# Moving the last value-sum copy ahead of the second layer-norm statistics, regrouping six SBUF tiles, and spreading the top-k over one more cycle

## The reference

```python
xn = _layernorm(x)                                  # first norm
# attention: a second norm with weights, then q, k, v, rotary, softmax, output projection
zn = (xn - mu) * rsqrt(var + LN_EPS) * ln_w + ln_b
q, k, v = rope(proj(zn, Wq, bq)), rope(proj(zn, Wk, bk)), proj(zn, Wv, bv)
attn = softmax(q @ k.T / sqrt(16)); a = xn + (attn @ v) @ Wo.T + bo
# experts: each takes the 256 rows per batch that score highest for it
gating, index = top_k(softmax(xn @ gate_w).T, 256)  # per batch and expert
h = silu(xn[index] @ Wg) * (xn[index] @ Wu)
f = scatter_add((h @ Wd) * gating)
return x + a + f
```

## Time and profile before

| | us |
|---|---|
| median of three runs | 1722.32 |
| lowest, highest | 1722.04, 1726.52 |
| the profiled execution's own time | 1719.68 |
| its span (first to last instruction) | 1717.5 |

### The profile page before, as it was taken

One profiled execution on the slowest core, in us unless ns is written; L12 is line 12 of the kernel. 1 busy time (PEld: TensorE's weight loads), 2 busy tenths in 40 slices (PEclk: granted clock), 3 DMA queues, 4 the chain that ended last, 5 costly groups with the idle time before them and its releaser, 6 DMA issues.

```text
span 1717.5 us, 29029 instructions
## 1 busy us (share of the span) xinstructions
PE 1668.0 (97%) x11128; PEld 946.9 (55%) x11128; DVE 1076.3 (63%) x2351; ACT 1190.9 (69%) x1416; POOL 510.1 (30%) x479
## 2 busy tenths in 40 slices
PE   5799999999999999999999999999999999999997
PEld 4234344334434433433434433368888888888886
DVE  8875486487567467568458658966545555454543
ACT  4698988998898899899898899953333333333322
POOL 3121111101201111112112100046565665656553
PEclk9899999999999999999999999999999999999999
DMA  5635745764674475465465466255353453535332
GB/s 168 175 89 124 140 108 118 173 130 106 156 160 109 120 165 138 108 149 142 118 148 127 113 128 140 46 162 125 68 98 63 93 100 57 99 59 96 65 56 31
DMA packets 113987, 196.08 MB, mean 114 GB/s; under 512 B 20896, under 2 KB 59680, under 8 KB 113696
## 3 DMA queue, kind: packets, MB, share of 16 engines
q1 hardware_dynamic: 83696, 143.01, 36.0%
q0 software_dynamic: 29040, 49.83, 14.9%
q10 hardware_dynamic: 1088, 1.05, 0.2%
HBM read 117.27 MB, written 76.55 MB: 113 GB/s over the span
## 4 chain that ended last, share of the span: by engine, by line
PE 88%; DVE 7%; DMA 2%; issue 1%; POOL 1%; SPq 0%; ACT 0%; DVEq 0%; POOLq 0%; ACTq 0%
PE o_ps L999 26%; PE score L1079 20%; PE score L985 18%; PE side L868 5%; PE score L1091 5%; PE o_ps L1091 3%; PE side L878 3%; PE side L1091 2%; PE side L909 2%; PE score L1066 2%; DVE stats L1128 1%; PE side L852 1%; DMA o_sums<-o_sb 1%; DVE o_sb L1471 1%; DMA probs<-in_wo_t 1%
## 5 line engine op out<-in xcount | busy, mean ns | idle before, releaser
L777 ACT ACTIVATE probs<-score 128x1024 f32<-128x1024 f32 x1024 | 968.6, 1053 | 107.6 <-PE score L985 105.3
L999 PE MATMUL o_ps<-probs,v_ones 128*32 128x512 f32 x4096 | 523.8, 604 | 8.7 <-DVE o_sb L1471 8.6
L985 PE MATMUL score<-q_stack,k_stack 50*128 50x512 f32 x2048 | 391.5, 455 | 4.0 <-issue 3.4
L985 PEld LDWEIGHTS score<-q_stack,k_stack 50*128 50x128 f32 x2048 | 162.8, 185 | 347.9 <-ACT probs L777 305.8
L761 ACT ACTIVATE probs<-score 128x512 f32<-128x512 f32 x128 | 76.5, 598 | 331.1 <-PE score L1079 331.1
L689 POOL DMA_INDIRECT out<-probs,rot x128 | 203.3, 1588 | 211.3 <-DVE probs L1436 182.0
L1421 DVE TENSOR_TENSOR probs<-score,probs 128x512 f32<-128x512 f32 x128 | 88.6, 692 | 209.9 <-PE score L1079 183.1
L999 PEld LDWEIGHTS o_ps<-probs,v_ones 128*32 128x32 f32 x4096 | 92.2, 108 | 209.8 <-issue 139.8
L667 POOL TENSOR_TENSOR square<-qk 128x512 bf16<-128x512 f32 x56 | 77.2, 1407 | 388.1 <-DVE qk L1274 388.1
L1079 PE MATMUL score<-k_stack,q_stack 128*128 128x512 f32 x640 | 158.6, 390 | 0.0
L678 POOL DMA_INDIRECT qk<-xn_rows,rot x128 | 134.0, 1047 | 38.4 <-issue 29.3
(11 more groups left out here) (282 smaller groups left out, 2548.0 us busy)
## 6 DMA issues: line engine op xcount, KB each, us to landing
q_parts<-parts SPq DMA_DIRECT2D x16, 1024.0 KB, 4.3
k_parts<-parts SPq DMA_DIRECT2D x16, 1024.0 KB, 7.4
q_stack<-q_parts SPq DMA_DIRECT2D x62, 256.0 KB, 7.0
k_stack<-k_parts SPq DMA_DIRECT2D x62, 256.0 KB, 8.8
q_stack<-q_parts SPq DMA_DIRECT2D x66, 128.0 KB, 7.2
k_stack<-k_parts SPq DMA_DIRECT2D x66, 128.0 KB, 7.6
o_sums<-o_sb SPq DMA_DIRECT2D x256, 32.0 KB
num<-o_sums SPq DMA_DIRECT2D x32, 256.0 KB
```

Of the source, the lines that this page charges most:

```text
L777: act.activation(probs[probs_of(b, s)][:, 2 * i:2 * i + 2, :], score[ring_of(b, p)][:, :, :], ACT.Exp, scale=SCALE).then_inc(exp_done, 1)
L985: last = pe.matmul(score[ring_of(b, p)][:, w, :], k_stack[par][rows, i, kt * P:(kt + 1) * P], q_stack[par][rows, i, qh * HALF:(qh + 1) * H ...
L999: last = pe.matmul(o_ps[j * KEYS_W:(j + 1) * KEYS_W, :], v_ones[par][:, kt, j, :], probs[probs_of(b, s)][:, j, :], start=kt == 0, stop=kt ...
```

## The change

1. The declarations of `zn_hi`, `zn_lo` and `v_sb` change places, so that `zn_hi`, `zn_lo`, `parts0`, `parts1` lie directly before the stacks. `zn_hi` then begins at byte 100192 of a partition, `zn_lo` at 108384, `parts0` at 116576, `parts1` at 124768. `qk`, `rot`, the `square` tiles and `v_sb` move down. The stacks, `v_ones`, `probs` and all behind them stay.
2. The second statistics become a function of their own, `stats2`. In cycle 0 of a batch with a predecessor and a successor (six of the eight), copy 7 comes between the scaling and `stats2`. Elsewhere the order is as before.
3. In the last batch the top-k operations of cycles 20 to 26 go from 5, 5, 5, 5, 4, 4, 2 to 5, 5, 4, 3, 4, 5, 4, and the job `lists` goes from cycle 27 to 28.

```diff
-    zn_hi, zn_lo = sb("zn_hi", [P, DC, S], F32R), sb("zn_lo", [P, DC, S], F32R)
...
+    v_sb = sb("v_sb", [P, KT, D])
+
+    zn_hi, zn_lo = sb("zn_hi", [P, DC, S], F32R), sb("zn_lo", [P, DC, S], F32R)
     parts = [sb(f"parts{i}", [P, NPART, 2, HALF], F32R) for i in range(2)]
-    v_sb = sb("v_sb", [P, KT, D])
-
     q_stack = [sb(f"q_stack{i}", [P, NPAIR, S], F32R) for i in range(2)]
...
-    LAST_JOBS = {0: ("top",), 9: ("wo", 0), 15: ("wo", 1), 23: ("wo", 2), 27: ("lists",), 30: ("wo", 3)}
+    LAST_JOBS = {0: ("top",), 9: ("wo", 0), 15: ("wo", 1), 23: ("wo", 2), 28: ("lists",), 30: ("wo", 3)}
...
-    TOPS_OF_CYCLE = (0, 5, 5, 5, 4, 4, 4, 0, 0, 4, 4, 5, 5, 5, 0, 3, 5, 4, 0, 4, 5, 5, 5, 5, 4, 4, 2, 0, 0, 0, 0, 0)
+    TOPS_OF_CYCLE = (0, 5, 5, 5, 4, 4, 4, 0, 0, 4, 4, 5, 5, 5, 0, 3, 5, 4, 0, 4, 5, 5, 4, 3, 4, 5, 4, 0, 0, 0, 0, 0)
...
             scaled(to, of, mv1, rstd1, xn_ready)
+
+        def stats2(n, th):
+            u = 2 * n + th
+            to = late_xn if u == 1 else xn
             dve.wait_ge(xn_ready, u + 1)
             stats_of(n, to, mv2, stats2_done)
             dve_n.end()
...
                     norm1(nxt, 0)
                     norm2(nxt, 0)
+                    if prev is not None:
+                        copy_o(prev, 2 * NG - 1)
+                    stats2(nxt, 0)
                 if c % 4 == 0 and c > 0:
                     copy_o(b, c // 4 - 1)
-                elif c == 0 and prev is not None:
+                elif c == 0 and nxt is None:
                     copy_o(prev, 2 * NG - 1)
...
                     elif c == 9:
                         norm2(nxt, 1)
+                        stats2(nxt, 1)
```

More of the change, by code:

```diff
@@ L1607, in _ @@
         norm2(0, 0)
+        stats2(0, 0)
         norm1(0, 1)
@@ L1612, in _ @@
         norm2(0, 1)
+        stats2(0, 1)
         dve.wait_ge(zeros_set, 2)
```

## The result

The changed kernel takes 1713.09 us (median of 6 executions, 1712.33 to 1715.89), the kernel before 1723.31 us on the same chip: ratio 0.9935, 95% interval 0.9920 to 0.9949. Run again beside other kernels it took 1712.59 us against 1723.49 us, ratio 0.9942 (0.9928 to 0.9956). The forecast was 1719.9 us and 2.4 us of gain; measured are 10 to 11 us. The time lies in the range given (1712.5 to 1723.0), near that of the rival *Nearer is faster* (1713.7), but the likeliest case was not what happened.

What follows compares the result with a forecast made beforehand. In attention ACT's idle time was taken to count, with PE setting the pace in heavy cycles; in the experts PE alone. Terms -2.25 - 0.65 + 0.5 + 0 = -2.4 us gave 1719.9 us, range 1712.5 to 1723.0.

Steps and rivals of the forecast that it cites:

- Nearer is faster: Rival (0.30) on expert and projection products: operands closer in address run faster, 6.2 us more gain, 1713.7 us.
- the likeliest case: The forecast itself for the whole kernel: 1719.9 us, own range 1718.5 to 1721.5, chance 0.47.
- Term: 0: Moved tiles in expert and projection products: their new place changes no pace, 0 us, bounds -6.2 and +5.6.
- The first rival: Another name for Nearer is faster (0.30): 4.5 us from 16 expert units and 1.7 us from projections.
- -2.25 us: Copy 7 at batch starts: the earlier copy closes five idle gaps on ACT, 2.25 us in all.
- the price: Batch starts: statistics and work behind them come 1.1 to 1.4 us later, costed at nothing, covered by DVE's idle time.
- -0.65 us: Top-k in the last batch: copy 5 starts 1.05 us earlier and ACT's 0.65 us gap goes.
- +0.5 us: Gathers before `turn(0)`: merged lists come 3.42 us later, PE stalls between 0 and 1.1 us, half taken.
- The gathers are late: Rival (0.12) at `turn(0)`: slow landing and slower issue make the stall 1.1 to 2.5 us, 1720.5 to 1721.9 us.
- -0.15 us: Top-k and list job together in the last batch: -0.65 us on ACT plus +0.5 us for the gathers.
- Farther is slower: Rival (0.07) on projections and down products: operands moved farther apart slow them by 5.6 us, 1725.5 us.
- nothing moves on ACT: Rival (0.04) in attention: ACT's gaps have another cause and stay despite the copy's new place, 1722.3 us or slightly more.

Runs made afterwards that it cites:

- parts0_off32: The changed kernel with parts0 alone 32 bytes off (100160), zn_hi and zn_lo in step above it; a unit of an even expert cost 0.18 us more.
- copy7_only: The kernel before with copy 7 ahead of the second statistics and nothing else; 1718.26 us against 1723.49, ratio 0.9969.
- zn_aligned_low: The changed kernel with zn_hi at byte 71520, a multiple of 4096 bytes below the gathered rows; a unit of an even expert took 10.91 us.
- zn_off32_high: The changed kernel with zn_hi, zn_lo, parts0 and parts1 32 bytes lower (zn_hi at 100160); a unit of an even expert took 11.20 us.
- order_only: The changed kernel with the tiles laid as before, so only the new orders of copy 7, top-k and lists; 1719.14 us against 1722.13, ratio 0.9978.
- tops_only: The kernel before with only the top-k operations and list job moved as in the change; 1723.95 us against 1723.49, ratio 1.0005.

## Why the prediction failed, point by point

**The sum.** Medians against the kernel before on the same chip, and fastest against fastest execution (1720.28 and 1720.23 us for the kernel before), in us:

| kernel | median | fastest |
|---|---|---|
| tiles alone | -4.1 | -4.5 |
| copy 7 alone | -5.2 | -2.9 |
| copy 7 and top-k | -3.0 | -3.1 |
| top-k alone | +0.5 | +0.6 |
| tiles and copy 7 | -10.4 | -7.9 |
| the change | -10.9 | -7.7 |

The kernel before was executed 20 and 23 times, the others 5 to 12 times, so its fastest is a little favoured. By fastest executions the parts add: -4.5 - 2.9 = -7.4, against -7.7 to -7.9 measured. The medians of the change give 3 us more, which the forecast had nowhere, and they don't add as well: -4.1 - 5.2 = -9.3.

**Tiles: the failed step.** "Term: 0" with bounds of -6.2 and +5.6; measured -4.1 to -4.5. The step took the row that shares an address: `parts0` slow at 108384, and `zn_lo` put there. After the change `zn_lo` is there and takes 390 ns. `parts0` had been in step and was slow by its company, as `parts0_off32` shows for other tiles. The second row, the projections at 395 ns, misled as well: the group is out of step before and after, and reads 395 ns in both, so it could not tell near from far. The first rival took the same group for a gain of 1.7 us; the batches of the trace became only 0.1 us shorter each by the tiles (135.85 in `copy7_only`, 135.76 after), so its time, 1713.7 us, came out by luck: its mechanism fell with `zn_aligned_low` and `zn_off32_high`, its 1.7 us for the projections did not come, and a surplus in the medians that it did not have, in part the clock's, took their place. The ratio of 10.91 to 11.19 us was the right row, and 16 x 0.28 = 4.5 us was its right price.

**The rule of the Trainium skill** (SBUF — State Buffer, "SBUF: two separate sides"), by which PE has ports of its own, gives nothing for a tile's place and agreed with my 0. The measured 0.28 us a unit come from an offset between two operands of PE itself, of which that section says nothing.

**Copy 7.** "-2.25 us": right in place and mechanism, short in size. The copy follows its `weigh` within 0.1 us, the gaps are gone, waits fell to 1.5 us. ACT's idle stretches over 0.15 us in batches 1 to 6 sum to 85.4 us before and 83.1 us in `copy7_only`: 2.3 us, the term to 0.1. The batches gained 2.9 us, the other 0.6 in stretches that I had not counted. Missing is the second effect of the same pause, the half clock, of which the trace of before shows no case between 100 and 1100 us. The median of `copy7_only` fell by 2.3 us more than its batches explain. Its fastest executions lack that surplus, and the mean clock rose from 0.9917 to 0.9921. On 1720 us that is 0.4 of a stretch, about 1 us. Executions of one clock, 0.992, are 3.8 us apart (1722.2 and 1718.4 us, seven of each), which leaves the clock some 1.4 of the 5.2 us. Where the rest of the surplus lies was not settled, and it isn't always there: `order_only` has the early copy 7 too and gained 3.0 us in the median and 3.1 by fastest executions. The cover that the price rested on held: nothing behind the statistics came late for ACT.

**Top-k and lists.** "-0.65 us" for ACT: right, the last batch is 0.86 us shorter (121.36, then 120.50). "+0.5 us" for the gathers: the wait was 1.34 us after the change, 1.51 in `tops_only` and 1.71 in `order_only`, above the upper bound of 1.1, and 1.07, just below it, when the changed kernel was profiled again. The step failed on the issue time: it kept the 4.93 us of before from POOL's copy (L675) to the issue of the last gather for unit 0, and it took 5.95, since the first two took 1.65 and 1.45 us on POOL where they had taken 1.10 and 1.09. The rival *The gathers are late* named this. The sum of the part, -0.15 us, is within what was measured (-0.5 and +0.5), by more luck than working.

**Farther is slower** and **nothing moves on ACT** did not happen: a unit's down products kept their 6.02 to 6.03 us, and the gaps closed.

**The median.** I carried the 2.6 us between the profiled execution and the median of three over to the changed kernel. They were not a constant of the kernel: before, the median lies 3.3 us above the fastest of 20 executions, after the change 0.1 us above the fastest of 5 and, in the first measurement, 0.8 above the fastest of 6.

## What to carry to other kernels

When the same products run at two paces, list the address of both operands of each, and take the distances modulo a power of two before thinking of near and far; here a distance of a multiple of 256 bytes between weights and moving rows made products of 512 columns 2.5% shorter, and one tile out of step slowed its neighbours; for the down products of 256 columns no gain was shown. A pause of PE in mid-kernel is to be priced twice, for itself and for the half clock that may follow it, which shows in the median of many executions rather than in one trace. A copy that PE waits for goes ahead of work that nobody waits for yet.

## What the hardware showed that I had not expected

- A product of 512 columns takes 227 ns (10.91 us for 48) with weights in step with the rows and 233 ns (11.19 us) without.
- Stretches of 3.41 or 6.83 us at 1.2 GHz stood behind some of PE's waits of 1.5 to 2.7 us and made a batch 1.6 to 3.0 us longer. Nine of the sixteen traces also have one at 77 to 82 us, in the first batch, at a wait of PE of 1.49 to 1.96 us; with 3.41 us of it that batch takes 135.3 to 135.5 us against 133.9 before. Six of the other traces have a wait of 1.15 to 1.44 us there and no such stretch; at `turn(0)` a wait of 1.71 us had none either.
- POOL took 0.95 to 1.80 us to issue a gather of the same size. The long ones around 1120 us (1.55 us before, 1.65, 1.45 and 1.80 after) stood beside DVE's casts and splits of weights, but so did one of 0.95 us before, at 1119.88; what makes them long was not tested.
